# Shifted attention scores contracted over 128 array rows instead of 98, with two more zero fills of the operand stacks

## The reference, cut to what matters

```python
scores = jnp.einsum('bhqd,bhkd->bhqk', q, k) * HD ** 0.5
attn = jax.nn.softmax(scores, axis=-1)
```

## Time and profile before

| | |
|---|---|
| median of 3 runs | 403.2 us (402.7 to 411.72) |
| the profiled execution, own time | 405.5 us |
| its span, first to last instruction | 403.7 us |
| mean granted TensorE clock | 0.918 |
| busy: PE, DVE, ACT, POOL | 320.5, 322.4, 201.6, 126.5 us |

### The profile page before, as it was taken

One profiled execution on the slowest core, in us unless ns is written; L12 is line 12 of the kernel. 1 busy time (PEld: TensorE's weight loads), 2 busy tenths in 40 slices (PEclk: granted clock), 3 DMA queues, 4 the chain that ended last, 5 costly groups with the idle time before them and its releaser, 6 DMA issues.

```text
span 403.7 us, 6180 instructions
## 1 busy us (share of the span) xinstructions
PE 320.5 (79%) x1634; PEld 251.7 (62%) x1634; DVE 322.4 (80%) x625; ACT 201.6 (50%) x373; POOL 126.5 (31%) x116
## 2 busy tenths in 40 slices
PE   0043379488948796878897897999999999999994
PEld 0032258275937585654575676888888888888882
DVE  6989888966897676777467997888888888888883
ACT  3131405262444255467455564666666666666651
POOL 1509424162032002011232333434334334334331
PEclk9999559657976998997899999999999999999999
DMA  5964906800680177300444445465555665655631
GB/s 175 165 172 148 157 9 176 139 1 21 168 132 0 53 151 115 106 8 28 141 138 125 153 172 173 161 188 192 193 185 194 192 184 191 199 182 188 192 140 52
DMA packets 33055, 55.10 MB, mean 136 GB/s; under 512 B 5206, under 2 KB 13830, under 8 KB 32010
## 3 DMA queue, kind: packets, MB, share of 16 engines
q1 hardware_dynamic: 33034, 54.85, 50.1%
HBM read 47.55 MB, written 5.52 MB: 131 GB/s over the span
## 4 chain that ended last, share of the span: by engine, by line
PE 48%; DVE 12%; issue 3%; ACT 3%; DMA 2%; POOL 1%; DVEq 0%; SPq 0%; ACTq 0%
PE ps L1266 7%; PE ps L1268 6%; PE ps L1277 6%; PE ps L1267 6%; PE ps L1278 6%; PE ps L1279 6%; PE ps L1179 3%; DVE q_st L959 2%; DVE scan L1052 2%; DMA k_st<-qk_split 2%; PE ps L1139 2%; DVE mx L806 1%; PE ps L1158 1%; DVE qk_lo L1057 1%; PE ps L1128 1%
## 5 line engine op out<-in xcount | busy, mean ns | idle before, releaser
L457 POOL TENSOR_TENSOR scan<-scan 128x512 f32<-128x512 f32 x68 | 73.3, 1078 | 136.9 <-ACT scan L584 135.2
L1057 DVE TENSOR_TENSOR qk_lo<-scan,qk_hi 128x512 fp32r<-128x512 f32 x68 | 69.3, 1019 | 30.6 <-ACT qk_hi L591 30.6
L584 ACT ACTIVATE scan<-ps 128x512 f32<-128x512 f32 x68 | 40.7, 599 | 49.1 <-PE ps L1268 48.9
L1277 PE MATMUL ps<-qk_hi,k_st 128*128 128x512 f32 x136 | 54.4, 400 | 4.5 <-DVE qk_lo L1057 4.3
L1266 PE MATMUL ps<-hid_hi,k_st 128*128 128x512 f32 x136 | 54.1, 398 | 2.0 <-DVE q_st L959 2.0
L577 ACT ACTIVATE k_st<-clip 128x512 fp32r<-128x512 f32 x68 | 42.8, 631 | 24.3 <-PE ps L1279 24.3
L1268 PE MATMUL ps<-hid_hi,q_st 128*128 128x512 f32 x136 | 53.8, 395 | 0.0
L1267 PE MATMUL ps<-hid_lo,k_st 128*128 128x512 f32 x136 | 53.4, 393 | 0.0
L806 DVE TENSOR_REDUCE mx<-ps 128x2 f32<-128x512 f32 x64 | 42.5, 684 | 13.5 <-PE ps L1139 12.2
L1278 PE MATMUL ps<-qk_lo,k_st 128*128 128x512 f32 x136 | 53.3, 392 | 0.0
L1279 PE MATMUL ps<-qk_hi,q_st 128*128 128x512 f32 x136 | 53.2, 391 | 0.0
(11 more groups left out here) (120 smaller groups left out, 490.2 us busy)
## 6 DMA issues: line engine op xcount, KB each, us to landing
clip<-in_tiles SPq DMA_DIRECT2D x68, 256.0 KB, 3.1
ex<-gates SPq DMA_DIRECT2D x136, 128.0 KB, 2.9
q_st<-qk_split SPq DMA_DIRECT2D x16, 256.0 KB, 4.5
k_st<-qk_split SPq DMA_DIRECT2D x32, 128.0 KB, 5.6
qk_split<-qk_hi SPq DMA_DIRECT2D x8, 256.0 KB, 2.2
qk_split<-qk_lo SPq DMA_DIRECT2D x8, 256.0 KB, 2.2
f_sb<-in_fT SPq DMA_DIRECT2D x4, 256.0 KB, 10.6
x_sb<-in_xT SPq DMA_DIRECT2D x4, 256.0 KB, 9.6
```

What stands on the lines that cost most here:

```text
L457: g.tensor_tensor(sq[:, k], relu[:, k], relu[:, k], ALU.mult).then_inc(sq_ready, 1)
L1057: TT(act_lo[:, k], act[:, k], act_hi[:, k].bitcast(F32), ALU.subtract).then_inc(act_lo_ready, 1)
L1277: mm(acc, w_hi, act_hi[:, k], start=first, stop=False, skip_group_check=True)
```

## The change

Two more DMAs fill rows 98 to 127 of `q_st` and of `k_st` with zeros from partitions 0 to 29 of `fill`; they stand right behind the three fills that exist. The shifted scores take all 128 rows of both stacks. PE's wait for the fills counts five DMAs instead of three (16 each).

```diff
@@ the fills, SP, batch 0
                     for st, r0, r1 in ((q_st, STACK, MAXROW), (k_st, STACK, MAXROW), (k_st, MAXROW, MAXROW + 2)):
                         sp.dma_start(st[r0:r1].rearrange("p n h s -> p (n h) s").bitcast(F32),
                                      fill[r0:r1].unsqueeze(1).broadcast_to([r1 - r0, SLOTS * HB, S])).then_inc(ld_fill, 16)
+                    for st in (q_st, k_st):
+                        sp.dma_start(st[MAXROW + 2:P].rearrange("p n h s -> p (n h) s").bitcast(F32),
+                                     fill[0:P - MAXROW - 2].unsqueeze(1).broadcast_to([P - MAXROW - 2, SLOTS * HB, S])
+                                     ).then_inc(ld_fill, 16)
@@ shifted_scores
-                    last = mm(bank_t(n)[:, kt], k_st[0:MAXROW + 2, slot(b, h // HB), h % HB, kt * P:(kt + 1) * P],
-                              q_st[0:MAXROW + 2, slot(b, h // HB), h % HB, :], start=True, stop=True)
+                    last = mm(bank_t(n)[:, kt], k_st[:, slot(b, h // HB), h % HB, kt * P:(kt + 1) * P],
+                              q_st[:, slot(b, h // HB), h % HB, :], start=True, stop=True)
@@ before the first scores
-            pe.wait_ge(ld_fill, 48)
+            pe.wait_ge(ld_fill, 80)
```

## The result

The changed kernel takes 411.52 us (median of 4, 410.48 to 414.76) where before takes 404.35 (median of 4); the ratio is 1.0205, with a 95% interval of 1.0117 to 1.0293. A second series gave 411.79 against 406.17, ratio 1.0175 (1.0121 to 1.0228). So it is slower, by about 2%; whether by more than 2% the intervals leave open. 408.4 was forecast, and both medians lie within 402 to 413.

A forecast was written before the change was run, and what follows sets the result against it. The head bounds the start of attention through DVE's clips(1), with PE and DVE each busy about four fifths of the span. Median 403.2 with head +6.2, SP and rows 0, clock -1.0 gives 408.4 us; range 402 to 413.

The forecast's parts named there:

- The bound and the cover: Head: a late clips(1) on DVE delays the whole attention; f_sb of batch 1 landed 1.7 us before its use.
- The fills' duration: Two new fills, 1.475 MB at 186 GB/s, take 7.9 us ahead of the inputs; 5.1 and 11.3 kept as ends.
- head term: Start of clips(1) and first scores: later by 7.9 - 1.7 = 6.2 us, 3.4 to 9.6 by the ends.
- the loads into few rows: Load of k_st into 16 rows at a time, 42 to 44 us: 131 GB/s, giving 11.3 us for the fills.
- The rival of slow fills: Fills run at 131 GB/s, 11.3 us: head +9.6, clock -1, total 411.8 us; chance 0.18.
- the 218 of the halved ports: Rows 98 to 127 reach 8 of 16 ports, 218 GB/s: pair 6.8 us, head term 5.1; not taken as hard limit.
- SP: Loads and unity queued behind the fills on SP would still precede store_qk(0): cost nothing.
- PE's wait: ld_fill of 80 instead of 48, met by about 31.9 us, before scores(0, 0) at 46.88: cost nothing.
- The rows' price: Shifted-score matmuls over 128 rows instead of 98: 128 x 0 ns, bound 0.6 us either way.
- The clock: PE stretches at 85 to 95, 125 to 130, 190 to 195 us: earlier high clock gains 1 us, bounds 8.6 gain, 2 loss.
- The sum: Profiled execution 405.5 + 6.2 + 0 + 0 - 1.0 = 410.7; the same terms against the median 403.2 give 408.4 us.
- the forecast case: The prediction's main case, total time 405.5 to 411.3 us, chance 0.52.

The follow-up runs named there:

- the timed pairs: Four kernels with 128-row shifted scores, each against its 98-row counterpart (ScalarE, the change, GpSimd, fills moved back): ratios lower by 0.0015, 0.0026, 0.0035 and 0.0042.
- The fills alone: The changed kernel with its two new fills kept but the shifted scores over 98 rows as before: median 416.25 us, ratio 1.0231 to before.
- the fills behind the inputs: The changed kernel, 128 rows, with its two new fills moved behind gate_bias in the queue: 405.41 us, ratio 1.0038; its 98-row control 407.9 us, 1.008.
- fills behind and keep_busy: The 128-row kernel with its new fills moved behind gate_bias, and keep_busy over 128 rows too: 405.79 us, ratio 1.0024 to before.

## Why the prediction was right

**The bound and the cover.** "The margin is 1.7 us. It is the cover of the new fills": held. DVE's wait is the delay of `f_sb` less that margin, 11.3 - 1.7 = 9.6, measured 9.5. One sign came otherwise: `f_sb` was to take some 23 us to land and took 18.7, because its issue itself moved from 8.52 to 16.58.

**The fills' duration** is the term that was mis-sized: 7.9 us forecast, 11.3 measured (8.7 in the second profile), so a head term of 9.5 and 6.8 instead of 6.2. It was worked out from the queue's 186 GB/s in 14 to 20 us. The trace of before had the lower rate for the taking, in the 4 us ahead of that stretch, with a queue just as full (last two columns: DMA share, GB/s):

```profile
10.00:12.00 2.00, 0.00 (x0) 0.00 (x0) 2.00 (x5) 0.81 (x2) 2.00 (x2) 1.00 1.05 129
12.00:14.00 2.00, 0.00 (x0) 0.00 (x0) 2.00 (x5) 0.00 (x0) 2.00 (x3) 1.00 1.12 138
```

Their mean of 133 GB/s gives 11.1 us for the pair. A reading of the 186 that fits: it counts all bytes, also those of later loads that some engines had already begun while others were still at the fills. After the change the queue again moves about as much, in the stretch 24 to 31 us

```profile
24.00:31.00 7.00, 5.06 (x16) 4.16 (x16) 1.10 (x2) 0.63 (x1) 0.00 (x0) 1.00 1.13 174
```

and up to the landing of `f_sb` 180 GB/s in 35.3 us, 6.35 MB, had moved, where before had 180 in 24.0, 4.32 MB. The difference of 2.03 MB is 0.56 more than the fills' 1.475: more of the later loads. No trace shows the engines one by one. For the landing the pair went at 1.475 MB / 11.3 us = 131 GB/s, the end of the range that I had from the loads into few rows. The rival of slow fills had the head right (+9.6). The 287 GB/s of 38 to 40 us, which the prediction held against the 218 of the halved ports, is no test of them: the store of `qk_lo` (issued at 37.21, 2.2 us to land) moved in it too.

**SP** had the last DMA ahead of q and k (`unity`) issued at 32.88 (29.3 forecast), ahead of the store at 40.77: no cost, as said. **PE's wait** cost nothing: the idle time before the first scores ends with the load of `k_st`.

**The rows' price** is nothing, as said: 0.43 and 0.24 us a pair.

**The clock** had the right sign, and a size that fits what can be told: 1 us forecast; 0.6 to 1.7 by the timed pairs, none of them clear by itself; 1.9 and 4.4 between the profile of before and those of the change. Its reason is right in part at most. The change's profile has 10.3 us less at 0.50 than before's: 6.9 in the stretch from 74.5 us on, where I expected it, and 3.4 at the end. The fills alone, with 98 rows, had the first part too, so in the changed kernel the later place of the attention is enough for it, and the full rows show only at the end of the attention, where for a while no other scores run. With the fills behind the inputs it is the other way round: there the first part came and the second didn't. What the clock follows in either place isn't shown.

**The sum.** 9.5 - 4.4 = 5.1 us of span; forecast 5.2. Two errors of 3 us cancelled in this profile, by luck. In the medians, +7.2 and +5.6 us, the head weighs more and the clock less. Both medians, 411.52 and 411.79, lie in the stated range but just above the 411.3 at which the forecast case ends: what came is the slow fills (411.8, chance 0.18), and the range held because it reached into them.

## What to carry to other kernels

A one-time fill isn't free because it is early: ask what stands behind it in the same queue, when that lands and when it is wanted; here 1.7 us of cover met 9 to 11 us of transfer. Take the time of a transfer from landings, not from the GB/s of a busy queue, and don't divide a copy into few partitions by its bytes: here 16 rows held up the next load about as long as 30. And don't read a gain of 1% from one profile each; time the pair. To pad an operand, let an engine write it that is idle and shares nothing with the busy one: ScalarE did it for nothing, GpSimd made the head 5.5 us longer.

## What I had not expected of the hardware

- GpSimd memsets of 32 x 2048 (1.9 us each) made VectorE's `tensor_scalar` of 128 x 4 last 1.24 us instead of 0.17.
- Fills into 16 rows, 0.79 MB, delayed the next load by 10.2 us, those into 30 rows, 1.47 MB, by 8.7 to 11.4.
- At the end of the attention kernels with 98-row shifted scores ran up to 17.0 us at a granted clock of 0.50 with PE busy 15.92 of them (four of five profiles; not before's own, which had 20.5 us at 0.50 from 74.5 us on instead); those with 128 rows at most 6.8 us in one piece (fills behind and keep_busy, 181.3 to 188.1). What in the last half batch decides it wasn't taken apart.
